# The layer norms' inverse roots become a power instruction on GpSimd

## What is computed

```python
x = layernorm(x + attention(x))
xn = layernorm(x) * g + b
abel = gelu(xn @ aw1 + ab1) @ aw2 + ab2              # a dense hidden layer of 512
moe = sum over the 2 best of 6 experts of weight * (gelu(xn @ ew1 + eb1) @ ew2 + eb2)
nonabel = moe @ expm(g0) @ expm(g1) @ expm(g2) @ expm(g3)
gate = sigmoid(concat(abel, nonabel) @ gc_w + gc_b)
x = layernorm(x + x + abel * (1 - gate) + nonabel * gate)
layernorm(x) = (x - mean) / sqrt(var + 1e-5)
```

## Time and profile before

| what | value |
|---|---|
| times of three runs | 680.0, 680.1 and 682.2 us, median 680.1 us |
| span of the profiled execution | 680.5 us |
| busy: PE, DVE, ACT, POOL | 629.8, 513.4, 442.2, 505.5 us |
| busy shares: PE, DVE, ACT, POOL | 93%, 75%, 65%, 74% |
| last head of attention, up to its end | about 442 to 504 us |
| feed-forward sections 0, 1, 2, 3 | begin at about 510, 565, 601, 632 us |
| last section and end | from about 660 us |

### The profile page before, as it was taken

The page is one execution under the profiler, slowest core; times in us unless marked ns, Lnnn a source line. Parts: engine busy times, 40 slices in busy tenths (PEclk is TensorE's granted clock), DMA queues, the critical chain, the costliest instruction groups (busy, mean ns, idle before and its releaser), DMA issues. The chain is left out here.

```text
span 680.5 us, 9930 instructions
## 1 busy us (share of the span) xinstructions
PE 629.8 (93%) x3043; PEld 485.0 (71%) x3043; DVE 513.4 (75%) x1138; ACT 442.2 (65%) x617; POOL 505.5 (74%) x296
## 2 busy tenths in 40 slices
PE   5879999999999999999999999999966998989992
PEld 3647777777777777777777777777655896767761
DVE  3676888887977888888797788886778774785675
ACT  3536786676776668667677666867843666656671
POOL 8016898887888889898788888989986545466770
PEclk8988999999999999999999999999987998999997
DMA  7622322223322232222332223333000000000001
GB/s 200 140 47 48 79 62 47 47 47 70 71 47 46 48 78 63 48 47 47 69 71 47 47 48 70 70 88 116 0 1 0 2 1 1 0 17 0 15 0 31
DMA packets 29074, 33.72 MB, mean 50 GB/s; under 512 B 6977, under 2 KB 15970, under 8 KB 28898
## 3 DMA queue, kind: packets, MB, share of 16 engines
q1 hardware_dynamic: 29026, 33.14, 20.2%
HBM read 6.84 MB, written 1.05 MB: 12 GB/s over the span
## 5 line engine op out<-in xcount | busy, mean ns | idle before, releaser
L391 POOL TENSOR_TENSOR probs_l<-probs,probs_h 128x1024 fp32r<-128x1024 f32 (+1 forms) x160 | 348.2, 2190 | 96.3 <-ACT probs_h L438 49.7
L435 ACT ACTIVATE probs<-scores 128x1024 f32<-128x1024 f32 (+1 forms) x160 | 150.5, 941 | 117.7 <-PE scores L658 61.6
L690 PE MATMUL out_ps<-probs_h,v 128*128 128x512 f32 (+5 forms) x640 | 181.3, 367 | 2.3 <-POOL probs_l L391 1.8
L517 DVE TENSOR_REDUCE m_part<-max_ps 128x1 f32<-128x512 f32 x192 | 127.0, 682 | 51.3 <-PE max_ps L631 50.0
L438 ACT ACTIVATE probs_h<-scores 128x1024 fp32r<-128x1024 f32 (+1 forms) x160 | 149.9, 937 | 0.0
L1037 POOL TENSOR_TENSOR v<-hid,k 128x512 fp32r<-128x512 f32 x64 | 83.3, 1308 | 58.2 <-ACT k L1113 45.2
L657 PE MATMUL scores<-q,k 128*128 128x512 f32 (+1 forms) x320 | 123.1, 385 | 0.0
L690 PEld LDWEIGHTS out_ps<-probs_h,v 128*128 128x128 f32 (+1 forms) x640 | 97.6, 162 | 28.3 <-POOL probs_l L391 7.2
L658 PE MATMUL scores<-q,k 128*128 128x512 f32 (+1 forms) x320 | 117.5, 367 | 0.0
L690 PE MATMUL out_ps<-probs_l,v 128*128 128x512 f32 (+1 forms) x320 | 116.9, 365 | 0.0
L631 PE MATMUL max_ps<-k,q 128*128 128x512 f32 (+2 forms) x320 | 104.1, 399 | 10.1 <-DVE m_part L517 8.1
(11 more groups left out here) (230 smaller groups left out, 986.8 us busy)
## 6 DMA issues: line engine op xcount, KB each, us to landing
k<-qk SPq DMA_DIRECT2D x96, 128.0 KB, 2.3
q<-qk SPq DMA_DIRECT2D x96, 128.0 KB, 2.3
q<-m_turn SPq DMA_DIRECT2D x128, 0.5 KB
v_all<-L_ffn_ew SPq DMA_DIRECT2D x2, 768.0 KB, 8.1
probs<-L_attn_x SPq DMA_DIRECT2D x4, 256.0 KB, 4.3
pos<-positions SPq DMA_DIRECT2D x1, 1024.0 KB, 6.0
out<-v_all SPq DMA_DIRECT2D x4, 256.0 KB, 2.3
acc<-L_attn_Wqkv SPq DMA_DIRECT2D x6, 128.0 KB, 3.1
```

Source lines behind the costliest of these rows:

```text
L391: pool.tensor_tensor(probs_l[:, p % 2, :, lo:CH], probs[:, p % 2, :, lo:CH], probs_h[:, n % 3, :, lo:CH], ALU.subtract).then_inc(S["probs_ ...
L435: act.activation(probs[:, p % 2, :, lo:CH], scores[:, p % 2, :, lo:CH], ACT.Exp, scale=D ** -0.5).then_inc(S["probs_ready"], 1)
L517: dve.tensor_reduce(m_part[:, r, 2 + j:3 + j], max_ps[:, u % 2, :], AX.X, ALU.max).then_inc(S["tile_max_ready"], 1)
L690: last = pe.matmul(o_ps(h, c)[0:rows, lo:CH], v, pr, start=(p == PAIR0[c] and j == 0 and k == 0), stop=(p == PAIR0[c + 1] - 1 and j == 1 a ...
```

## The change

The guess and the Newton rounds leave DVE. POOL makes the inverse roots: it adds eps to the variances (for two roots per row with two TENSOR_SCALAR), waits for that, and raises the sums to the power -0.5 in one TENSOR_TENSOR with the operation `pow`, against a tile that holds -0.5 (a tile of -0.5 and one of eps are set at the program's start). DVE's writes wait for a semaphore that counts POOL's steps. The small numbers are all in SBUF (`ln_root`). PE's wait before it turns chunk 1's rows (slot 15 of the last head) is gone, since the scratch no longer lies in that bank.

The steps left are dealt out anew: in the last head DVE's statistics stand in slots 11 and 16, POOL's roots in slots 12 and 17, DVE's writes in slots 13, 14 and 18, 19. In section 0 the statistics end in slot 5, the roots stand in slot 6 behind hid_lo(6), and the writes in slots 8 to 15. In sections 1 to 3 the statistics stand in slots 12 and 13, the root behind hid_lo(13), the four writes in slot 15; in the last section the root stands at the end of POOL's program.

```diff
-NORM_STEPS = (3, 5, 5, 12)
+NORM_STEPS, LAST_ROOT_AT = (3, 6, 0, 4), 13
+REST_STEPS, REST_ROOT_AT = (3, 3, 3, 3, 3, 2, 0, 0, 2, 2, 2, 2, 2, 2, 2, 2), 6
-NORM_AT = {11: (0, 9), 12: (0, 9), 13: (0, 7), 14: (0, 5), 16: (1, 9), 17: (1, 9), 18: (1, 6), 19: (1, 6)}
+NORM_AT, ROOT_AT = {11: (0, 9), 13: (0, 4), 14: (0, 4), 16: (1, 9), 18: (1, 4), 19: (1, 4)}, {12: 0, 17: 1}
...
+                    if h * NP + p - (H - 1) * NP in ROOT_AT:
+                        c = ROOT_AT[h * NP + p - (H - 1) * NP]
+                        pool.wait_ge(S["power_made"], 2)
+                        pool.wait_ge(S["first_norms_steps"], c * both_steps(TPC) + statistics_steps(TPC))
+                        two_roots(pool, S["first_roots_steps"], ROOTS * c, early.ln, TPC)
...
-                        if c == 1:
-                            pe.wait_ge(S["first_norms_steps"], both_roots(TPC))
...
+    pool.tensor_scalar(root[:, 0:n], var, EPS, None, ALU.add).then_inc(sem, 1)
+    pool.tensor_scalar(root[:, n:2 * n], var, 1.0 + EPS, EPS * EPS, ALU.mult, ALU.add).then_inc(sem, 1)
+    pool.wait_ge(sem, base + 2)
+    pool.tensor_tensor(root[:, 0:2 * n], root[:, 0:2 * n], power[:, 0:2 * n], ALU.pow).then_inc(sem, 1)
...
     yield from statistics(dve, sem, base, src, buf, n)
-    base = base + 2 * n + 1
-    dve.wait_ge(sem, base)
-    dve.tensor_scalar(var, mean_var[:, 0:n, 1], EPS, None, ALU.add).then_inc(sem, 1)
-    yield
-    yield from inverse_root(dve, sem, base + 1, small)
+    dve.wait_ge(rooted, roots + 2)
...
+            def last_root(c):
+
+                _, mean_var, root, power, eps, _ = early.ln
+                pool.wait_ge(S["last_norm_steps"], ln_steps(TPC) * (c - 1) + statistics_steps(TPC))
+                pool.tensor_tensor(root[:, 0:TPC], mean_var[:, 0:TPC, 1], eps[:, 0:TPC], ALU.add).then_inc(S["last_root_ready"], 1)
+                pool.wait_ge(S["last_root_ready"], 2 * (c - 1) + 1)
+                pool.tensor_tensor(root[:, 0:TPC], root[:, 0:TPC], power[:, 0:TPC], ALU.pow).then_inc(S["last_root_ready"], 1)
...
+                    if not first and j == LAST_ROOT_AT:
+                        last_root(c)
```

More of the change, by code:

```diff
@@ L263, in attention @@
         block = ctx.enter_context(nc.Block())
[L265 to L269, removed]
         def group(n, hi):
@@ L549, in section @@
                         c, steps = NORM_AT[last]
-                        if last - 1 not in NORM_AT or NORM_AT[last - 1][0] != c:
+                        if last in NORM_BEGINS:
                             dve.wait_ge(S["early_x_loaded"], 16)
@@ L779, in layer_norm, with two_roots @@
[L779 to L788 removed]
+def two_roots(pool, sem, base, buf, n):
+    _, mean_var, root, power, _, _ = buf
+    var = mean_var[:, 0:n, 1]
+    pool.tensor_scalar(root[:, 0:n], var, EPS, None, ALU.add).then_inc(sem, 1)
+    pool.tensor_scalar(root[:, n:2 * n], var, 1.0 + EPS, EPS * EPS, ALU.mult, ALU.add).then_inc(sem, 1)
+    pool.wait_ge(sem, base + 2)
+    pool.tensor_tensor(root[:, 0:2 * n], root[:, 0:2 * n], power[:, 0:2 * n], ALU.pow).then_inc(sem, 1)
@@ L789, in layer_norm, with two_norms @@
+def layer_norm(dve, sem, base, rooted, roots, src, dst, buf, n):
+    _, mean_var, root, _, _, _ = buf
+    yield from statistics(dve, sem, base, src, buf, n)
+    dve.wait_ge(rooted, roots + 2)
     for i in range(n):
-        dve.tensor_scalar(dst[:, i, :], src[:, i, :], mean_var[:, i, 0:1], guess[:, i:i + 1],
+        dve.tensor_scalar(dst[:, i, :], src[:, i, :], mean_var[:, i, 0:1], root[:, i:i + 1],
                           ALU.subtract, ALU.mult).then_inc(sem, 1)
         yield
-def two_norms(dve, sem, base, src, once, twice, buf, n):
-    _, mean_var, small, _ = buf
-    var, guess = small[0], small[2]
+def two_norms(dve, sem, base, rooted, roots, src, once, twice, buf, n):
+    _, mean_var, root, _, _, _ = buf
@@ L802, in two_norms @@
     yield from statistics(dve, sem, base, src, buf, n)
[L803 to L809, removed]
+    dve.wait_ge(rooted, roots + ROOTS)
     for k, dst in enumerate((once, twice)):
         for i in range(n):
-            dve.tensor_scalar(dst[:, i, :], src[:, i, :], mean_var[:, i, 0:1], guess[:, k * n + i:k * n + i + 1],
+            dve.tensor_scalar(dst[:, i, :], src[:, i, :], mean_var[:, i, 0:1], root[:, k * n + i:k * n + i + 1],
@@ L899, in feed_forward @@
         gw, gb, gcb = early.gw, early.gb, early.gcb
[L900 to L911, removed]
         gen2_t = sb("gen2_t", [P, NROT, P])
@@ L1039, in section @@
                         add_to_series(SERIES_AT[j])
+                    if first and j == REST_ROOT_AT:
+                        pool.wait_ge(S["first_norms_steps"], 2 * both_steps(TPC) + statistics_steps(NT // 2))
+                        two_roots(pool, S["first_roots_steps"], 2 * ROOTS, early.ln, NT // 2)
+                    if not first and j == LAST_ROOT_AT:
+                        last_root(c)
             section(0, first=True)
@@ L1043, in _ @@
                 section(c)
+            last_root(NC)
         @block.scalar
@@ L1287, in section @@
                         dve.tensor_tensor(rot_lo[:], product(0)[:, 0, :], rot_hi[:], ALU.subtract).then_inc(S["rotation_low_ready"], 1)
-                    for _ in range(3 if first else 0):
-                        next(rest, None)
+                    for _ in range(REST_STEPS[j] if first else 0):
+                        next(rest)
                     if cur and j < NA:
@@ L1329, in section @@
                         dve.wait_ge(S["second_residual_ready"], c)
-                        norm = layer_norm(dve, S["last_norm_steps"], ln_steps(TPC) * (c - 1), last_sum, y2[:, ts, :], last_sums(second), TPC)
+                        norm = layer_norm(dve, S["last_norm_steps"], ln_steps(TPC) * (c - 1), S["last_root_ready"], 2 * (c - 1), last_sum, y2[:, ts, :], early.ln, TPC)
                     if prev and j >= T_NORM:
```

42 lines of the change are left out of this document (14 added, 28 removed).

## The result

The changed kernel takes 689.45 us (median of five runs, 684.75 to 690.35) where the kernel before takes 680.1 (680.0 to 682.2): a ratio of 1.0114 (95% interval 1.0092 to 1.0137). It is slower, and outside the range of 675.5 to 683.0. The profiled execution has a span of 688.6 us, 8.1 more than before's 680.5; its own time is 690.35. Among the five the shortest, 684.75 us, has the highest mean granted clock, 0.977, and the three near 690 have 0.963 to 0.966.

What follows compares the result with a forecast made beforehand. PE bounds most stages, PE and POOL the last head. Gains 3.3 + 0.3 + 0 + 2.0 - 0.6 = 5.0 us less 6p (p = 0.5) gave 2.0 us: 678.1 us, range 675.5 to 683.0.

Steps and rivals of the forecast that it cites:

- the sum: Whole kernel: gains of 5.0 us over the places minus 6p for the roots, 2.0 us gained with p = 0.5.
- I take p = 0.5: Assumed price in us of one power on POOL, between 0.2 and 0.74, with 0.2 and 2.4 as ends.
- the same for 4 and for 8 columns: Claim that a power on POOL has one price p, whether for single or double roots.
- in its shadow: Double roots: the second TENSOR_SCALAR runs behind the first at no cost, so a root occupies POOL for 0.3 + p.
- ACT and PE are fed by POOL and full themselves, so nothing is caught up: Last head: two roots among POOL's `probs_l` delay everything, a loss of 0.6 + 2p.
- predicted 2.0 - 1.01: Program's end: DVE's 2.46 us go, handovers, addition, wait and p come; gain 2.0 - p.
- The two MEMSETs at the start lie before the first loads arrive: Program's start: filling the new tiles was claimed to cost nothing.
- The end of section 1: DVE's late root steps vanish, both PE stalls go and layer2(0) starts earlier; gain 3.3 - p.
- The end of section 2: The root pushes hid_lo(14) by p, about 0.3 us comes back before layer2(0); gain 0.3 - p.
- Section 3: Its end: the root delays hid_lo(14) and the whole end follows, nothing to get back; gain 0 - p.
- the cover: Section 0: hid_lo(7) had 1.10 us idle before it and is needed three slots later, so the root costs nothing.
- the slow power: Rival: loss over 2 us from p = 1.2, 689.5 with p = 2.4; chance 0.22 including the code load.

Runs made afterwards that it cites:

- e1: Changed kernel with a multiplication where the power stood, same tiles and waits: 680.0 us, ratio 1.0005 to the kernel before.
- e6: Changed kernel with fourteen matrix products nobody reads, ahead of PE's two long waits (last head, layer2(14) of chunk 3): 685.6 us, ratio 1.0065.
- e11: Changed kernel with its three small tiles behind all others and unread products ahead of PE's two long waits: 682.8 us, ratio 1.0022.
- e10: Kernel before with the two fills on GpSimd at the start and two more semaphores, nothing moved: 680.0 us, ratio 0.9994.
- e8: Kernel before with an empty tile of 32 columns, moving later tiles by 128 bytes, no instruction added: 681.3 us, ratio 1.0018.
- e12: Changed kernel with its three small tiles behind all others and nothing else: 685.3 us, ratio 1.0058.
- e9: Kernel before with a power only at the ends of section 1 and the program, small tiles behind all others, fills in the feed-forward part: 677.7 us.
- e4: Kernel before with a power on GpSimd only at the end of section 1 and at the program's end: 679.0 us, ratio 0.999.
- e2: Changed kernel with the last head's two double roots by Newton rounds on VectorE as before: 681.1 us, ratio 1.0017.
- e7: Changed kernel with multiplication for the power and five unread products ahead of PE's wait in slot 15, last head: 679.0 us, ratio 0.9977.

## Why the prediction was wrong

Three things failed, one in a term of the sum and two that the sum didn't have. The price alone turns the forecast gain into a loss of 2.4 us, 682.5, which is still inside the range; PE's clock and the moved tiles take the time out of it.

**The price.** The step that failed first is "I take p = 0.5", "the same for 4 and for 8 columns". Measured: 1.01 and 1.67 us, and with additions, waits and handovers a double root holds POOL from 483.77 (482.49 + 1.28, the end of `acc`) to 486.10, 2.3 us instead of 0.8. Of that, 0.65 us are not the power: the second TENSOR_SCALAR runs behind the first (484.17 and 483.85), not in its shadow, as the 0.3 us of the sum have it. With the measured powers alone the prediction's own formula makes 5.0 - 4 x 1.01 - 2 x 1.67 = -2.4, a loss, 682.5 us. Neither row that served as a neighbour knew it: a plain operation on the same 8 columns takes 0.205 us (e1), an eighth of the power. The Trainium skill (GPSIMD Engine Reference, section 4.1, Engine selection) has plain elementwise work on GpSimd about twice as slow as on VectorE, which the prediction weighed as an estimated 0.34 us. This does not carry over to a power: 1.01 us was measured, about six times the 0.17 of a small step on DVE.

**PE's clock.** "ACT and PE are fed by POOL and full themselves, so nothing is caught up" was right, and the sum stopped there: it took PE's products behind a longer wait at their old length. In the profile slots 12 to 19 lose 7.2 us, of which the two roots are 2.3 each; 2.1 more come at one step, between slots 15 and 16, where `probs_l`'s lag behind the profile of before goes from 4.8 to 6.9 us with the clock at 0.50. At the program's end a gain of 1.06 us in the norm came (predicted 2.0 - 1.01), but 3.35 us went on the way to it. e6 and e11 show that both are PE's idle time: with the waits filled, the clock behind them stays at 1.00 and 2.7 us come back in the last head; at the end 1.8 come back in e6, and in e11, where the clock stays up longer, all of it. The Trainium skill (TensorE: Matmul & The Clock Gate, Part 1) says that PE's clock is set by how busy PE has been recently, with 1.2 GHz for an idle and 2.4 GHz for a busy PE. The windows of this case agree, with 0.50 behind waits of 3.31 and 1.51 us and 1.00 where the same waits were filled. The prediction had read PE's wait of 1.01 us and not asked what a longer one does.

**Moved tiles.** "The two MEMSETs at the start lie before the first loads arrive" was right of the fills (e10: no loss), and left out the tiles that they fill. These are allocated ahead of attention's tiles and move them; e8 loses 2.1 us by that alone, e12 and e9 lose nothing of it.

The rest, place by place, with the measured p put in. The end of section 1: predicted a gain of 3.3 - 1.0 = 2.3, measured 2.5; PE's wait of 0.84 us there is the root's price, which the sum has by counting from the end of hid_lo(14). The end of section 2: predicted a loss of 0.7, measured 0.3. By itself that would prove nothing, since e4 and e9 lose 0.7 there without any root on POOL; beside e1, which gains 0.4 there, the root's price is seen. Section 3: predicted a loss of 1.0, measured 0.8. Section 0: against the profile of before, hid_lo(6) starts 8.6 us late, hid_lo(7) behind the root 11.2 and hid_lo(10) 8.7. The 2.5 us that the root adds are gone three blocks later: the cover held, though this root has 16 columns and a power of 2.94 us.

Of the rivals the slow power came true, at the places that it named ("mainly the last head and the end of section 3"), but not by its price: 689.5 was worked out with p = 2.4, and came with p between 1.0 and 1.7, a clock and moved tiles: that the number is met is chance. Nor does a run show its reason, a chain of dependent steps; the runs show a price that grows with the columns. No call loads code: the first power takes 1.68 us, the second 1.67.

The sum of the profile: 2.4 for the roots at their measured price, 2.0 for the tiles from head 1 on, 2.1 and 3.35 for the clock make 9.9; the stretches at half clock at the beginnings of sections 0 and 1, which fall otherwise, gave back 0.7 and 1.5. That leaves 7.6, and the span is 8.1 longer; 0.5 us are not accounted for. Two things stay open: which idle times of PE the clock falls behind, there and elsewhere; and which property of an address it is that PE's reads depend on.

## What to carry to other kernels

Before work is moved to an engine that another one waits for, work out how long the waiting engine then stands idle: behind waits of PE of 1.5 to 3.3 us, stretches at half clock cost, besides the wait, 2.1 us in the last head and 3.35 at the end of the changed kernel, though not behind every such wait. An operation that no row shows has no price, and a neighbour with the same shape may be eight times off; measure it alone, at the width that it will have. Put new small tiles behind the large ones, and take a change apart by place: the two places out of six where a DVE stall really ended last are worth 2.3 us by themselves (e9; 0.9 to 3.7), all six together lose 7.8 by the ratio.

## What the runs showed of the hardware

A power on POOL costs 1.01, 1.67 and 2.94 us for 4, 8 and 16 columns of 128 partitions, about 0.16 us for each further column, where a multiplication takes 0.20 to 0.22 at all three widths (e1). Moving PE's operands by 128 bytes in SBUF (e8, and e1, e2, e6 and e7 with the changed kernel's places) lengthens its 128x512 products by 2 ns of 393, on three chips alike. And fourteen products that nobody reads, in time in which PE stood idle, shorten the kernel by 3.3 us (e6).
